# First expert layer as three float32r products with its weights loaded and split per tile, three query buffers, and written-out expert loops

## The chip, the cores and the metric

The kernel runs on one core of a Trainium2 chip. Its engines are TensorE (PE in the profile, with PEld for its weight loads), VectorE (DVE), ScalarE (ACT), GpSimd (POOL) and SyncE (SP), each with an instruction queue of its own that runs in order, and they meet at semaphores. The metric is the device time of one execution in microseconds, the median of three runs. All times below are microseconds (us) unless another unit stands with them.

## What is computed

One transformer layer on x of 4096 rows by 256, with an attention and a mixture of eight experts, of which each row takes two:

```
h = layernorm(x) * (1 + ca) + sa
x = x + ga * attention(h)              # 16 heads of 16; key <= query + 128
h = layernorm(x) * (1 + cb) + sb
scores = h @ gate_w + gate_b           # 8 experts, the top 2 of each row
hid = relu(einsum('td,edf->etf', h, W1) + b1[:, None, :])   # 256 -> 1024
y = einsum('etf,efd->etd', hid, W2) + b2[:, None, :]        # 1024 -> 256
x = x + gb * einsum('te,etd->td', combine, y)
```

All inputs are float32. W1 and W2 hold eight experts of 1 MB each.

## The kernel before

The program runs five stages one after the other: attention_inputs with the projections (to about 130 us), score_shifts and row_maxima (to 193), attention (to 1284), route (to 1460) and experts (to 2046), and then a copy of the sums to the output.

**attention** goes over 32 tiles of 512 queries: four groups of four heads (g), eight tiles each, r counting both. SP loads a tile's queries (load_stack into q_rows, two halves by turns, L983 to L985), then waits on q_in until they have landed (L986), and at tile 3 of a group loads the keys of the next group (L987 to L990). Before the load of tile r it waits for `turned` of tile r-2 (L983). TensorE makes scores of keys and queries (L1009), later the products of probabilities and values (L1026), and, one tile behind, four transposes of the finished output (L1038), which raise `turned`. ScalarE takes the exponentials (L1107), GpSimd cuts the edge of the mask (L1092), VectorE copies and divides.

**route** goes over eight chunks of 512 rows: normalise, score, choose two experts, count each row's place in its expert's queue, and scatter the normalised rows (rt_xs, L1473) to a queue in DRAM, eight scatters a chunk. SP's load() brings the chunk's attention output and x, stores sums, and loads a share of W1, one expert of 1 MB a chunk (L1279), which stays in SBUF for all eight experts; load_w2 brings W2. GpSimd adds the bias to x (L1343).

**experts** goes over 71 tiles of 128 queue rows, each of one expert. What each engine does for a tile t:

- SP: loads the tile of rows (value load L1715, DMA L1716), once the tile two before has been transposed and its meta columns have been read. The last three experts of W2 are loaded at the start of the stage (L1721).
- TensorE: first_layer(t) in fp32, two halves of 512 columns by two halves of the inner 256 (L1760; each fp32 product stands as two instructions, so eight rows); turn_rows(t+1), two transposes (L1750); second_layer(t-1), eight products (L1779); turn_hidden(t), eight transposes (L1771).
- VectorE: copies half of the hidden layer (L1853), modulates the transposed rows into xT (modulate, L1829), reads the meta columns of the row tile (read_meta, L1838 to L1845: the row's share and where its answer goes, four steps on one column), and makes the answer (L1858 to L1871: denominator, reciprocal, output plus bias b2, times share and gate).
- ScalarE: one exponential (L1808), the other half of the hidden layer (L1811), eight relu (L1814).
- GpSimd: scatter-adds the answer to the sums in DRAM (L1739). A scatter waits for the one before to have landed.

The loops over tiles are hardware loops (over_queue, with Fori, two tiles a pass). The order on each engine is the order of the code.

Of the kernel before, what the change touches and what calls it, by code (L numbers as in the profile page):

```python
# [857 lines left out]
def attention(nc, dram, keep):  # L858

    with ExitStack() as ctx:  # L860
# [21 lines left out]
        q_rows = sb("at_q_rows", [STACK, 2 * GH * C], BF16)  # L882
# [11 lines left out]
        q_in = sem("at_q_in")  # L894
# [77 lines left out]
        def _(sp):  # L972
# [5 lines left out]
            for r in range(TILE_COUNT):  # L978
                g, tile = r // NC, r % NC
                half = r % 2  # L980

                if r >= 2:
                    sp.wait_ge(turned, r - 1)  # L983
                load_stack(sp, q_rows[:, half * GH * C:(half + 1) * GH * C].rearrange("r (h s) -> r h s", h=GH),
                           dram["q_parts"], Q_TERM, slice(g * GH, (g + 1) * GH), slice(tile * C, (tile + 1) * C), q_in)  # L985
# [5 lines left out]
            sp.wait_ge(k_in, G * K_IN)  # L991

        @block.tensor
        def _(pe):
            def scores(g, tile, n, c):
# [3 lines left out]
                k_at, q_at = (g % 2) * GH * S, ((g * NC + tile) % 2) * GH * C  # L999
# [63 lines left out]
            for c, (g, tile, n) in enumerate(order):  # L1063
                if n == 0:
                    if tile == 0:
                        pe.wait_ge(k_in, (g + 1) * K_IN)
                    pe.wait_ge(q_in, (g * NC + tile + 1) * Q_IN)
# [63 lines left out]
def route(nc, dram, keep):  # L1131
# [6 lines left out]
    with ExitStack() as ctx:  # L1138
# [117 lines left out]
        W1_SHARE = E // NC  # L1256
# [5 lines left out]
        def _(sp):  # L1262
# [5 lines left out]
            def load(c, u, it):  # L1268
# [378 lines left out]
def experts(nc, dram, keep):  # L1647


    with ExitStack() as ctx:  # L1650
# [6 lines left out]
        def sem(name):  # L1657
            return ctx.enter_context(nc.semaphore(name))

        ident, mod_cols, w1, w2, b1, b2, owner = (  # L1660
            keep[n] for n in ("ident", "mod_cols", "w1", "w2", "b1", "b2", "owner"))
# [10 lines left out]
        xT = sb("ex_xT", [P, KD, P], F32)  # L1672
        h = sb("ex_h", [P, FF * P], F32)
# [9 lines left out]
        w2_in = sem("ex_w2_in")  # L1683
        x_turned = sem("ex_x_turned")
# [15 lines left out]
        def over_queue(eng, body, done=0):  # L1700

            with eng.Fori(done, (TILES - 1) // 2) as it:
                for u in range(2):
                    body(it * 2 + (u + 1), (u + 1) % 2, it)

        @block.sync
        def _(sp):
            sp.sem_inc(x_turned, 2)

            def load(tile, u):  # L1710

                sp.wait_ge(x_turned, tile + 1)
                if not isinstance(tile, int) or tile >= 2:
# [8 lines left out]
            load(2, 0)  # L1722
            over_queue(sp, lambda tile, u, it: load(tile, u), done=1)
            load(TILES, TILES % 2)
            sp.wait_ge(x_in[TILES % 2], 16 * ((TILES + 1) // 2))
# [7 lines left out]
        def _(pool):  # L1733
            for tile in range(TILES):
                pool.wait_ge(y_ready, tile + 3)
# [9 lines left out]
        def _(pe):  # L1745
# [7 lines left out]
            def first_layer(tile):  # L1753
                e = pe.value_load(owner[0:1, bass.ds(tile, 1)], min_val=0, max_val=E - 1)
                pe.wait_ge(xT_ready, tile + 2)
                for i in range(HALVES):

                    pe.wait_ge(h_copied[i], tile + 1)
                    for k in range(KD):
                        ins = nc.tensor.matmul(ps_h[i][:], xT[:, k, :],  # L1760
                                               w1[:, bass.ds(e, 1), k, i * C:(i + 1) * C].rearrange(
                                                   "p a f -> p (a f)"), start=k == 0, stop=k == KD - 1)
                    ins.then_inc(hidden[i], 1)
                return e
# [196 lines left out]
```

## Time and profile before

| | |
|---|---|
| median of three runs | 2066.1 us (2063.37 to 2066.82) |
| the profiled execution | 2067.55 us |
| its span, first to last instruction | 2065.8 us |
| TensorE busy | 1828.7 us (89% of the span) |
| ScalarE busy | 1337.1 us (65%) |
| VectorE busy | 466.4 us (23%) |
| GpSimd busy | 290.1 us (14%) |
| exponentials of attention, L1107 | 1023.4 us busy, 756 of them |
| second layer, L1779 | 258.7 us busy, 1136 rows |

Busy shares are means over five stages that differ, so the profile is read stage by stage: the busy times of a stretch tell which engine never stops there, the timeline of one tile tells how long each step takes and what released it, and the chain of waits tells what stood on the path that ended last. In a timeline row the columns are start, duration, engine, line, operation, output and inputs, shape and count; the bracket gives the engine's idle time ahead of the row and what ended it. A granted clock (PEclk) of 1.00 is TensorE's full speed.

### The profile page before, as it was taken

Reading aid. Unit: us, or ns where it says so; the run is one execution under the profiler, and the core shown is the slowest. Engines: PE = TensorE matmul, PEld = TensorE weight load, DVE = VectorE, ACT = ScalarE, POOL = GpSimd, SP = SyncE. Lnnn points to the kernel's source line nnn. Section 1 sums busy time; section 2 is a strip of 40 time slices with the busy share of each in tenths; the row PEclk is TensorE's granted clock in tenths of the full one; section 3 lists DMA queues with packets and bytes.
Section 4 is the critical chain, followed back from the end, with each engine's and each line's share of the span. In section 5 each row is a group of like instructions: output and inputs, shape, how many; then the busy total and the mean of one; then the engine's idle time right before and its main releaser. Section 6 shows DMA issues by size and latency. Waiting matters only on the chain. (4 is left out here: it accounts for less than half of the span.)

```text
span 2065.8 us, 47120 instructions
## 1 busy us (share of the span) xinstructions
PE 1828.7 (89%) x18425; PEld 949.3 (46%) x18426; DVE 466.4 (23%) x1368; ACT 1337.1 (65%) x1649; POOL 290.1 (14%) x333
## 2 busy tenths in 40 slices
PE   4944999999999999999999998664599999999995
PEld 3832333333333333333333332554376767666673
DVE  4954000000000000000000000445133333333331
ACT  3723999998899989999899998222233333333331
POOL 1000101001000010000111000356112121212111
PEclk8975999999999999999999999765799999999998
DMA  4464400003100003000000000962412122122223
GB/s 138 155 158 101 88 10 10 10 10 66 40 10 10 10 17 81 18 9 10 15 20 18 10 2 10 347 247 83 122 31 34 33 33 33 33 33 33 33 33 97
DMA packets 84274, 116.10 MB, mean 56 GB/s; under 512 B 9484, under 2 KB 76108, under 8 KB 83532
## 3 DMA queue, kind: packets, MB, share of 16 engines
q1 hardware_dynamic: 67064, 90.97, 15.5%
q0 software_dynamic: 13296, 17.80, 5.0%
q10 hardware_dynamic: 3760, 5.03, 0.9%
q8 instruction: 126, 2.06, 0.4%
q14 instruction: 28, 0.23, 0.0%
HBM read 73.03 MB, written 40.74 MB: 55 GB/s over the span
## 5 line engine op out<-in xcount | busy, mean ns | idle before, releaser
L1107 ACT ACTIVATE at_probs<-at_scores 128x1536 f32<-128x1536 f32 (+2 forms) x756 | 1023.4, 1436 | 62.7 <-PE at_scores L1009 57.4
L1009 PE MATMUL at_scores<-at_q_rows,kept_k_rows 99*32 99x512 bf16 (+3 forms) x9920 | 621.1, 363 | 38.3 <-ACT at_probs L1107 16.9
L1026 PE MATMUL at_out<-at_probs,kept_v 128*17 128x512 f32 (+3 forms) x4832 | 587.9, 565 | 5.0 <-DVE at_out_T L1120 4.9
L1009 PEld LDWEIGHTS at_scores<-at_q_rows,kept_k_rows 99*32 99x32 bf16 x9920 | 239.6, 97 | 564.3 <-ACT at_probs L1107 342.3
L1814 ACT ACTIVATE ex_hT<-ex_ps_hT,kept_b 128x128 f32<-128x128 f32 x568 | 154.2, 383 | 376.0 <-PE ex_ps_hT L1771 376.0
L1779 PE MATMUL ex_ps_y<-kept_w,ex_hT 128*128 x1136 | 258.7, 381 | 2.4 <-ACT ex_hT L1814 2.4
L1760 PE MATMUL ex_ps_h<-kept_w,ex_xT 128*128 x568 | 259.9, 601 | 0.9 <-DVE ex_xT L1829 0.9
L1120 DVE COPY at_out_T<-at_out 128x512 f32<-128x512 f32 x32 | 22.1, 692 | 972.1 <-PE at_out L1026 972.1
L1092 POOL TENSOR_SCALAR_AFFINE_SELECT at_probs<-at_probs 128x512 f32<-128x512 f32 (+2 forms) x156 | 83.0, 541 | 1014.7 <-ACT at_probs L1107 1013.3
L1779 PEld LDWEIGHTS ex_ps_y<-kept_w,ex_hT 128*128 128x128 f32 x1136 | 211.7, 191 | 28.6 <-issue 2.7
L1026 PEld LDWEIGHTS at_out<-at_probs,kept_v 128*17 128x17 f32 x4832 | 127.9, 98 | 130.3 <-DVE at_out_T L1120 19.9
L1739 POOL DMA_INDIRECT sums<-ex_y,ex_answer_to x71 | 110.7, 1560 | 486.9 <-DVE ex_y L1871 486.9
L1760 PEld LDWEIGHTS ex_ps_h<-kept_w,ex_xT 128*128 128x128 f32 x568 | 104.2, 194 | 105.8 <-issue 105.8
L1853 DVE COPY ex_h<-ex_ps_h 128x512 f32<-128x512 f32 x71 | 49.2, 692 | 229.5 <-PE ex_ps_h L1760 229.5
L1771 PE MATMUL ex_ps_hT<-kept_ident,ex_h 128*128 128x128 f32 x568 | 74.5, 275 | 0.0
L1353 POOL DMA_INDIRECT queue<-rt_xs,rt_row_int x64 | 65.6, 1026 | 56.5 <-DVE rt_row_int L1585 39.5
L1771 PEld LDWEIGHTS ex_ps_hT<-kept_ident,ex_h 128*128 128x128 f32 x568 | 67.3, 142 | 7.0
L1829 DVE TENSOR_SCALAR ex_xT<-ex_ps_x,kept_mod_cols 128x128 f32<-128x128 f32 x144 | 51.9, 403 | 21.3 <-PE ex_ps_x L1750 21.3
L1392 PE MATMUL rt_ps_o<-rt_wo,rt_aT 128*128 128x256 f32 x128 | 45.5, 533 | 9.1 <-ACT rt_aT L1463 9.1
L1750 PE MATMUL ex_ps_x<-kept_ident,ex_x_tile 128*128 128x128 f32 x144 | 28.1, 277 | 28.5 <-DMA ex_x_tile<-queue 24.7
L1750 PEld LDWEIGHTS ex_ps_x<-kept_ident,ex_x_tile 128*128 128x128 f32 x144 | 20.5, 144 | 66.2 <-issue 61.6
L1811 ACT COPY ex_h<-ex_ps_h 128x512 f32<-128x512 f32 x71 | 45.0, 634 | 4.2 <-PE ex_ps_h L1760 4.2
(220 smaller groups left out, 963.0 us busy)
## 6 DMA issues: line engine op xcount, KB each, us to landing
kept_w<-in_W SPq DMA_DIRECT2D x16, 1024.0 KB, 11.3
ex_x_tile<-queue SPq DMA_DIRECT2D x72, 129.5 KB, 2.1
k_parts<-kparts SPq DMA_DIRECT2D x8, 768.0 KB, 3.7
q_parts<-qparts SPq DMA_DIRECT2D x8, 768.0 KB, 3.7
at_q_rows<-q_parts SPq DMA_DIRECT2D x32, 192.0 KB
kept_k_rows<-k_parts SPq DMA_DIRECT2D x4, 1120.0 KB
x_rows<-in_x SPq DMA_DIRECT2D x4, 1024.0 KB, 13.9
kept_k_rows<-k_parts SPq DMA_DIRECT2D x8, 512.0 KB
```

Of the source, the lines that this page charges most:

```text
L1009: ins = nc.tensor.matmul(ps_s[b:b + CT, c % 2, at:at + part], k_rows[:, k + b:k + b + CT], q_rows[:, q:q + part], start=True, stop=True)
L1026: ins = nc.tensor.matmul(ps_o[h * CT:h * CT + HD + 1, first:C], v[:, kb, g * GH + h, :], probs[:, slot, column:column + width], start=i == ...
L1092: nc.gpsimd.affine_select(out=part, in_=part, compare_op=ALU.is_ge, fill=0.0, base=0, pattern=pattern, channel_multiplier=-1).then_inc(mas ...
L1107: nc.scalar.activation(probs[:, c % RING, 0:width], ps_s[:, c % 2, 0:width], ACT.Exp).then_inc(exped, 1)
L1353: pool.indirect_dma_start(dram["queue"], bass.IndirectOffsetOnAxis(ap=row_int[:, u, j, i:i + 1], axis=0), xs[:, u, j, :], None).then_inc(s ...
L1739: pool.indirect_dma_start(dram["sums"], bass.IndirectOffsetOnAxis(ap=answer_to[:, tile:tile + 1], axis=0), y[:, tile % 2, :], None, comput ...
L1760: ins = nc.tensor.matmul(ps_h[i][:], xT[:, k, :], w1[:, bass.ds(e, 1), k, i * C:(i + 1) * C].rearrange("p a f -> p (a f)"), start=k == 0, ...
L1771: ins = nc.tensor.transpose(ps_hT[:, f, :], h[:, f * P:(f + 1) * P], ident[:])
L1779: ins = nc.tensor.matmul(ps_y[u][:, 0:D], hT[:, f, :], w2[:, bass.ds(e, 1), f, :].rearrange("p a d -> p (a d)"), start=f == 0, stop=f == F ...
L1814: nc.scalar.activation(hT[:, f, :], ps_hT[:, f, :], ACT.Relu, bias=b1[:, bass.ds(e * FF + f, 1)]).then_inc(rectified, 1)
L1829: ins = nc.vector.tensor_scalar(xT[:, k, :], ps_x[:, k * P:(k + 1) * P], mod_cols[:, 6 + k:7 + k], mod_cols[:, 4 + k:5 + k], ALU.mult, ALU ...
L1853: nc.vector.tensor_copy(h[:, C:2 * C], ps_h[1][:]).then_inc(h_copied[1], 1)
```

## The change

Three things are changed.

1. attention has three query buffers with a semaphore each. SP waits, from the fourth tile on, for the scores of the tile that last read the buffer (`scored`), in place of the transposes, and no longer waits after each load that it has landed. The load of the next group's keys, which stands behind the load of tile 3 on SP, is no longer behind that wait either.
2. route no longer loads W1, and W1 has no room of its own for all experts.
3. experts loads the W1 of a tile's expert anew for each tile, into two buffers, and splits it on chip: ScalarE rounds it to float32r (w1_high), VectorE and GpSimd subtract that from the full weights, half each (w1_low). The rows are split the same way on VectorE (xT_high, xT_low); modulate moves to ScalarE. The first layer is then, for each half of the columns, high by high, high by low and low by high, twelve float32r products of 512 columns in place of four fp32 ones. The loops over tiles are written out.

The core of the diff:

```diff
-                if r >= 2:
-                    sp.wait_ge(turned, r - 1)
...
-                sp.wait_ge(q_in, (r + 1) * Q_IN)
+                u = r % Q_BUFFERS
+                if r >= Q_BUFFERS:
+                    done = r - Q_BUFFERS + 1
+                    sp.wait_ge(scored, chunk_base(done // NC, done % NC))
...
                 if tile == 3 and g + 1 < G:
 
                     sp.wait_ge(k_in, (g + 1) * K_IN)
                     load_keys(g + 1)
...
-                share = bass.ds(c * W1_SHARE, W1_SHARE)
-                sp.dma_start(keep["w1"][:, share].rearrange("p e k f -> p (e k) f"),
-                             dram["W1"][share].rearrange("e (k p) f -> p (e k) f", p=P)
-                             ).then_inc(keep["weights_in"], 16)
...
+            def load_w1(tile, u):
+                if tile >= 2:
+                    for k in range(KD):
+                        sp.wait_ge(w1_rest[k], tile - 1)
+                e = sp.value_load(owner[0:1, bass.ds(tile, 1)], min_val=0, max_val=E - 1)
+                sp.dma_start(w1[:, u], dram["W1"][bass.ds(e, 1)].rearrange("e (k p) f -> p (e k) f", p=P)
+                             ).then_inc(w1_in[u], 16)
+
+            load_w1(0, 0)
             load(0, 0)
             load(1, 1)
+            load_w1(1, 1)
             for e in range(E - 3, E):
...
+            for tile in range(2, TILES):
+                load(tile, tile % 2)
+                load_w1(tile, tile % 2)
...
+            def rest(tile):
+                pool.wait_ge(w1_rounded, tile + 1)
+                if tile >= 2:
+                    pool.wait_ge(hidden[HALVES - 1], tile - 1)
+                nc.gpsimd.tensor_tensor(w1_low[:, tile % 2, 1], w1[:, tile % 2, 1], w1_high[:, tile % 2, 1],
+                                        ALU.subtract).then_inc(w1_rest[1], 1)
+            rest(0)
+            rest(1)
             for tile in range(TILES):
+                if tile + 2 < TILES:
+                    rest(tile + 2)
                 pool.wait_ge(y_ready, tile + 3)
...
+                    for n, (x_part, w) in enumerate(((xT_high, w1_high), (xT_high, w1_low), (xT_low, w1_high))):
+                        for k in range(KD):
+                            ins = nc.tensor.matmul(ps_h[i][:], x_part[:, k, :], w[:, u, k, cols],
+                                                   start=n == 0 and k == 0, stop=n == 2 and k == KD - 1)
...
+            def round_w1(tile):
+                act.wait_ge(w1_in[u], (tile // 2 + 1) * 16)
+                if tile >= 2:
+                    act.wait_ge(hidden[HALVES - 1], tile - 1)
+                    for k in range(KD):
+                        act.wait_ge(w1_rest[k], tile - 1)
+                nc.scalar.copy(w1_high[:, u], w1[:, u]).then_inc(w1_rounded, 1)
...
                 nc.scalar.copy(h[:, 0:C], ps_h[0][:]).then_inc(h_copied[0], 1)
+                if tile + 1 < TILES:
+                    modulate(tile + 1)
+                if tile + 2 < TILES:
+                    round_w1(tile + 2)
                 act.wait_ge(h_turned, tile + 1)
...
+            def split_x(tile):
+                dve.wait_ge(xT_full, tile + 1)
+                if tile >= 1:
+                    dve.wait_ge(hidden[HALVES - 1], tile)
+                nc.vector.tensor_copy(xT_high[:], xT[:]).then_inc(xT_rounded, 1)
+                dve.wait_ge(xT_rounded, tile + 1)
+                nc.vector.tensor_tensor(xT_low[:], xT[:], xT_high[:], ALU.subtract).then_inc(xT_ready, 1)
...
                 copy_hidden(tile)
-                modulate(tile + 1)
-                if not isinstance(tile, int) or tile + 1 < TILES:
+                if tile + 1 < TILES:
+                    split_x(tile + 1)
                     read_meta(tile + 1, 1 - u)
+                if tile + 2 < TILES:
+                    rest(tile + 2)
                 answer(tile - 1, 1 - u)
```

The first rest(tile) above is GpSimd's, round_w1 is ScalarE's, split_x VectorE's. VectorE has a rest(tile) like GpSimd's, on the first half of the inner 256 and with w1_rest[0].

SP's queue in the expert loop, one tile, before (the value load and the DMA of the rows, then the loop's branch):

```order
L1715 TENSOR_LOAD kept_row_of_tile [waits ex_meta_read,ex_x_turned]
L1715 ISA x2
L1716 ISA
L1716 DMA ex_x_tile<-queue 128x259
L1702 UNCONDITIONAL_BRANCH
```

and after, the same tile (ex_w is the buffer of W1, kept_owner the expert of each tile):

```order
L1718 TENSOR_LOAD kept_row_of_tile [waits ex_meta_read,ex_x_turned]
L1718 ISA x2
L1719 ISA
L1719 DMA ex_x_tile<-queue 128x259
L1726 TENSOR_LOAD kept_owner [waits ex_w1_rest_1,ex_w1_rest_0]
L1726 ISA x2
L1727 ISA
L1727 DMA ex_w<-in_W 128x2x1024
```

Behind each load of rows now stands a load of weights with two waits of its own, and each load of weights stands behind the load of rows of the same tile.

VectorE's queue in the expert loop, one step, before (copy of the hidden half, modulate, the meta columns, then the answer):

```order
L1853 COPY ex_h<-ex_ps_h 128x512 [waits ex_hidden_1]
L1829 TENSOR_SCALAR ex_xT<-ex_ps_x,kept_mod_cols 128x128 [waits ex_x_turned]
L1829 TENSOR_SCALAR ex_xT<-ex_ps_x,kept_mod_cols 128x128
L1838 TENSOR_SCALAR ex_sign<-ex_x_tile,kept_owner_of 128x1
L1840 TENSOR_SCALAR ex_padding<-ex_x_tile,kept_spill 128x1
L1843 SCALAR_TENSOR_TENSOR ex_lead<-ex_sign,ex_x_tile 128x1 [waits ex_meta_step]
L1845 SCALAR_TENSOR_TENSOR ex_answer_to<-ex_padding,ex_x_tile 128x1
L1858 TENSOR_LOAD kept_owner [waits ex_meta_read]
L1858 ISA x2
L1861 TENSOR_SCALAR ex_den<-ex_grown 128x1 [waits ex_grown_ready]
```

and after:

```order
L1912 COPY ex_h<-ex_ps_h 128x512 [waits ex_hidden_1]
L1881 CAST ex_xT_high<-ex_xT 128x256 [waits ex_hidden_1,ex_xT_full]
L1883 TENSOR_TENSOR ex_xT_low<-ex_xT,ex_xT_high 128x256 [waits ex_xT_rounded]
L1897 TENSOR_SCALAR ex_sign<-ex_x_tile,kept_owner_of 128x1
L1899 TENSOR_SCALAR ex_padding<-ex_x_tile,kept_spill 128x1
L1902 SCALAR_TENSOR_TENSOR ex_lead<-ex_sign,ex_x_tile 128x1 [waits ex_meta_step]
L1904 SCALAR_TENSOR_TENSOR ex_answer_to<-ex_padding,ex_x_tile 128x1
L1889 TENSOR_TENSOR ex_w_low<-ex_w,ex_w_high 128x1024 [waits ex_hidden_1,ex_w1_rounded,ex_meta_read]
L1917 TENSOR_LOAD kept_owner
L1917 ISA x2
L1920 TENSOR_SCALAR ex_den<-ex_grown 128x1 [waits ex_grown_ready]
```

The two steps of modulate have left this queue, the split of the rows stands in their place, and the subtraction of the weights stands between the meta columns and the answer.

## Rows read from the trace of the kernel before

**Rows 1.** expert loop busy: us, PE, PEld, DVE, ACT, POOL, PEclk, DMA, GB/s

```profile
1482.00:2044.00 562.00, 559.55 (x2383) 391.25 (x2382) 213.88 (x768) 191.11 (x698) 109.19 (x70) 1.00 0.20 32
```

**Rows 2.** timeline, one tile's TensorE work in the expert loop

```profile
1688.86 0.38 PE L1750 MATMUL ex_ps_x<-kept_ident,ex_x_tile 128*128 128x128 f32 x2
...
1693.41 3.60 PE L1760 MATMUL ex_ps_h<-kept_w,ex_xT 128*128 x8
...
1696.85 0.38 PE L1750 MATMUL ex_ps_x<-kept_ident,ex_x_tile 128*128 128x128 f32 x2
```

**Rows 3.** timeline, TensorE's float32r products in the prologue

```profile
76.16 0.71 PE L345 MATMUL ps_q<-hT_high,wq_high 128*128 128x512 f32 x2
...
79.00 3.62 PE L356 MATMUL ps_v<-wv,hT 128*128 128x256 f32 x16
```

**Rows 4.** groups by line: busy and mean ns, idle time before

```profile
L576 ACT ACTIVATE sh_square_k<-sh_high_k 128x2048 bf16<-128x2048 bf16 x4 | 7.6, 1910 | 34.0 <-DMA sh_high_k<-k_parts 34.0
...
L443 DVE TENSOR_TENSOR hT_low<-hT,hT_high 128x1024 fp32r<-128x1024 f32 x8 | 9.8, 1219 | 7.2 <-ACT hT L280 7.2
```

**Rows 5.** timeline of the route stage, GpSimd and VectorE

```profile
1372.31 2.35 POOL L1343 TENSOR_TENSOR rt_x_now<-rt_x_now,rt_bo_gated 128x1024 f32<-128x1024 f32 x1
...
1372.50 0.19 DVE L1575 TENSOR_TENSOR rt_rank<-rt_ps_r,rt_queue_end 128x32 f32<-128x32 f32 x1 [2.01 <-PE rt_ps_r L1422]
...
1372.80 1.91 DVE L1581 TENSOR_TENSOR rt_equal<-rt_rank,kept_w 128x32 f32<-128x32 f32 x1
```

**Rows 6.** chain of waits, SP at the start of the experts

```profile
1459.28 0.27 SPq L1715
...
1460.01 0.37 SPq L1716
```

**Rows 7.** timeline, VectorE's and GpSimd's steps of a tile

```profile
1690.76 0.16 DVE L1843 SCALAR_TENSOR_TENSOR ex_lead<-ex_sign,ex_x_tile 128x1 f32 x1
...
1691.94 0.15 DVE L1861 TENSOR_SCALAR ex_den<-ex_grown 128x1 f32 x1 [0.91 <-DVE ex_answer_to L1845]
...
1692.95 0.42 DVE L1868 TENSOR_TENSOR ex_y<-ex_ps_y,kept_b 128x256 f32<-128x256 f32 x1 [0.66 <-PE ex_ps_y L1779]
...
1693.41 0.48 DVE L1871 SCALAR_TENSOR_TENSOR ex_y<-ex_y,ex_share,kept_gates 128x256 f32<-128x256 f32 x1
...
1694.17 1.57 POOL L1739 DMA_INDIRECT sums<-ex_y,ex_answer_to  x1 [6.42 <-DVE ex_y L1871]
```

**Rows 8.** page, DMA issues: count, KB each, median us to landing

```profile
ex_x_tile<-queue SPq DMA_DIRECT2D x72, 129.5 KB, 2.1
...
k_parts<-kparts SPq DMA_DIRECT2D x8, 768.0 KB, 3.7
...
sums<-ex_y,ex_answer_to POOLq DMA_INDIRECT x71, 3.8
```

**Rows 9.** one line's landings, L1721 (three loads of W2)

```profile
DMA to landing us min/median/max: 6.6/9.1/11.3
```

**Rows 10.** timeline of attention: first tile of groups 0, 1 and 3

```profile
207.09 7.00 ACT L1107 ACTIVATE at_probs<-at_scores 128x1536 f32<-128x1536 f32 x5 [1.00 <-PE at_scores L1009]
...
474.74 2.75 PE L1009 MATMUL at_scores<-at_q_rows,kept_k_rows 99*32 99x384 bf16 x56 [3.88 <-DMA at_q_rows<-q_parts]
...
476.27 2.79 ACT L1107 ACTIVATE at_probs<-at_scores 128x1536 f32<-128x1536 f32 x2 [5.70 <-PE at_scores L1009]
...
1023.81 2.80 ACT L1107 ACTIVATE at_probs<-at_scores 128x1536 f32<-128x1536 f32 x2 [4.96 <-PE at_scores L1009]
```

**Rows 11.** timeline of attention, behind a load of keys

```profile
521.27 1.04 PE L1009 MATMUL at_scores<-at_q_rows,kept_k_rows 99*32 99x512 bf16 x7 [2.93 <-issue]
```

**Rows 12.** busy times of the route stage, columns as in group 1

```profile
1284.00:1460.00 176.00, 94.74 (x497) 79.47 (x497) 78.56 (x303) 39.88 (x67) 87.02 (x83) 0.64 0.60 213
```

**Rows 13.** waits: us in total, times, longest

```profile
ACT rt_xs L1473 <- DMA queue<-rt_xs,rt_row_int: 41.5, 6, 10.5
```

**Rows 14.** chain of waits, last load of W2

```profile
1462.65 11.35 DMA kept_w<-in_W
```

More of the change, by code:

```diff
@@ L893, in attention @@
         k_in = keep["k_in"]
-        q_in = sem("at_q_in")
+        q_in = [sem(f"at_q_in_{u}") for u in range(Q_BUFFERS)]
         ready = sem("at_ready")
@@ L991, in _ @@
             sp.wait_ge(k_in, G * K_IN)
+            for u in range(Q_BUFFERS):
+                sp.wait_ge(q_in[u], Q_IN * len(range(u, TILE_COUNT, Q_BUFFERS)))
         @block.tensor
@@ L1683, in experts @@
         w2_in = sem("ex_w2_in")
+        w1_in = [sem(f"ex_w1_in_{u}") for u in range(2)]
+        w1_rounded = sem("ex_w1_rounded")
+        w1_rest = [sem(f"ex_w1_rest_{k}") for k in range(KD)]
+        xT_full = sem("ex_xT_full")
+        xT_rounded = sem("ex_xT_rounded")
         x_turned = sem("ex_x_turned")
@@ L1698, in experts @@
         block = ctx.enter_context(nc.Block())
[L1700 to L1704, printed above, removed]
         @block.sync
@@ L1791, in tile_steps @@
             def tile_steps(tile, u, it):
-                first_layer(tile)
-                turn_rows(tile + 1, 1 - u, it + 2)
+                first_layer(tile, u)
+                if tile + 1 < TILES:
+                    turn_rows(tile + 1, 1 - u, it + 2)
                 second_layer(tile - 1, 1 - u)
                 turn_hidden(tile)
-            over_queue(pe, tile_steps)
+            for tile in range(1, TILES):
+                tile_steps(tile, tile % 2, (tile - 1) // 2)
             second_layer(TILES - 1, (TILES - 1) % 2)
@@ L1815, in tile_steps @@
                                          bias=b1[:, bass.ds(e * FF + f, 1)]).then_inc(rectified, 1)
-            tile_steps(0)
-            over_queue(act, lambda tile, u, it: tile_steps(tile))
+            round_w1(0)
+            modulate(0)
+            round_w1(1)
+            for tile in range(TILES):
+                tile_steps(tile)
         @block.vector
@@ L1824, in _, with rest @@
             dve.sem_inc(y_ready, 2)
-            def modulate(tile):
-                dve.wait_ge(x_turned, tile + 3)
-                for k in range(KD):
-                    ins = nc.vector.tensor_scalar(xT[:, k, :], ps_x[:, k * P:(k + 1) * P], mod_cols[:, 6 + k:7 + k],
-                                                  mod_cols[:, 4 + k:5 + k], ALU.mult, ALU.add)
-                ins.then_inc(xT_ready, 1)
+            def split_x(tile):
[5 more added lines that the diff above has]
+                nc.vector.tensor_tensor(xT_low[:], xT[:], xT_high[:], ALU.subtract).then_inc(xT_ready, 1)
+            def rest(tile):
+                dve.wait_ge(w1_rounded, tile + 1)
+                if tile >= 2:
+                    dve.wait_ge(hidden[HALVES - 1], tile - 1)
+                nc.vector.tensor_tensor(w1_low[:, tile % 2, 0], w1[:, tile % 2, 0], w1_high[:, tile % 2, 0],
+                                        ALU.subtract).then_inc(w1_rest[0], 1)
             META = 3
@@ L1864, in answer @@
                 dve.wait_ge(out_done, tile + 1)
-                if not isinstance(tile, int) or tile >= 2:
+                if tile >= 2:
                     dve.wait_ge(y_added, tile * 16 - 16)
```

73 lines of the change are left out of this document (39 added, 34 removed).

## Prediction

> **What bounds the kernel now.** I read the stages first, then in the expert stage the engine that is never idle, then the gaps of the attention stage. In the expert loop TensorE is busy 559.55 of 562 us at a granted clock of 1.00, while VectorE, ScalarE and GpSimd are busy 214, 191 and 109 us [rows 1]. A tile takes 7.99 us (1688.86 to 1696.85), of which the first layer's eight fp32 passes take 3.44 (1693.41 to 1696.85) [rows 2]. So whatever shortens TensorE's row pays in full, until another chain of work takes longer than TensorE's row. The attention stage is bound by ScalarE's exponentials, which stop for 5 to 6 us at three places [rows 10].
>
> **First layer on TensorE.** Removed: 3.44 us a tile. Added: 12 float32r products on 512 columns. The prologue has the same form: 12 of them run from 76.16 to 79.00 [rows 3], 2.84 us. I take that; with 3.44 as the end at which nothing is gained, and no reason for less than 2.84. TensorE's own period becomes 7.99 - 3.44 + 2.84 = 7.39 us. The written-out loops issue the same TensorE work in the same order.
>
> **The new chain for weights.** W1 now comes once per tile, and a buffer is free for tile t+4 only when both subtractions for tile t+2 are done. GpSimd's subtraction stands ahead of a scatter and behind the last scatter on its queue, VectorE's ahead of the answer that the scatter needs. That closes a loop which returns after two tiles:
> scatter(t-1), GpSimd subtract(t+2), SP's load of x and of W1 for t+4, ScalarE's rounding(t+4), VectorE subtract(t+4), answer(t+1), scatter(t+1). Its links:
> - GpSimd subtracts 128x1024 in fp32: 2.35, as the same shape takes in the route stage [rows 5].
> - Before SP comes to W1 it must issue the x tile (the queue is in order), and that waits for read_meta, VectorE's [128x1] steps with two operands in SBUF. In the route stage a VectorE operation with two SBUF operands that began 0.49 after GpSimd's subtract took 1.91 and ended at 1374.71, 0.05 after GpSimd's end at 1374.66; its neighbour of the same 128x32 shape with one operand in PSUM took 0.19 [rows 5]. I take it that read_meta is held the same way: it ends 0.15 after the subtraction, one step of 0.16 without it [rows 7].
> - SP: 0.73 from the end of its wait to the issue of x, and 0.37 for the issue itself [rows 6]: 1.10; then 0.73 again up to the issue of W1.
> - Landing of 1 MB. No row shows this load. 129.5 KB take 2.1 and 768 KB take 3.7 [rows 8], which is 2.5 ns per KB and gives 4.4 for 1024 KB alone, the lower end. The upper end is 6.6, the first of three 1 MB loads of W2 in one burst [rows 9]. The loop's present traffic keeps the DMA engines 0.20 busy [rows 1], 1.6 us of a tile's 8; if half of it falls into the load, 0.8 more: 5.1 is my estimate, nearer to the lower end since no second large load is in flight with it.
> - ScalarE rounds 128x2048: 1.9, taken from a bf16 row of that shape; VectorE subtracts 128x1024: 1.22 [rows 4].
> - The answer: 0.35 for the denominator and its reciprocal, 0.94 for the two steps on y (1692.95 to 1693.89); 0.28 to the scatter's start and 1.57 for it [rows 7].
> - Six handovers between engines at 0.05, as at the held step's end [rows 5]: 0.3.
> Sum: 2.35 + 0.15 + 1.10 + 0.73 + 5.1 + 1.9 + 1.22 + 1.29 + 1.85 + 0.3 = 15.99 us for two tiles, **8.0 a tile**, against 7.99 now. The register load ahead of the answer shows 0.91 of idle time today [rows 7]; I cost it at nothing because the 1.22 of the subtraction ahead of it on VectorE covers it. Without that cover the loop is 16.9, 8.45 a tile, +31 us.
> So the 0.60 us that TensorE saves per tile I expect to be idle time on TensorE, and the loop to run at the pace of the weights. 68 tiles x 0.01 = +1 us.
>
> What else is moved in this stage: modulate goes to ScalarE (two 128x128 steps, about 0.7 in place of VectorE's), and the rounding stands on ScalarE's queue ahead of the eight relu of the same tile. If W1(t+2) is late, the relu wait behind it, and second_layer(t) behind them. ScalarE then has 191 / 70.3 = 2.7 us a tile of today [rows 1] plus 1.9 plus 0.7, 5.3 of 8; VectorE 3.0 of today, less 0.7, plus two steps of 0.48 or less for split_x (the 128x256 form of [rows 7]) and 1.22, and what it is held, under 7. Neither is the bound. The scatter itself waits for the rows of the scatter before, which land 3.8 after their issue [rows 8], well inside a period.
>
> "SBUF — State Buffer", section "Who interferes with whom", in the Trainium skill speaks against this change: a VectorE instruction with two SBUF inputs and a GpSimd instruction that reads SBUF exclude each other for the whole of an instruction, and the one that issued first keeps the port. The trace agrees for 128x32 (1.91 in place of 0.19), and no run here shows it for a 128x1 step. By that rule the loop is 8.0 a tile; were the small steps exempt, it would be the 7.39 of the first rival.
>
> **Attention.** SP loads the queries of a group's first tile only after the transposes of two tiles before, and at three boundaries TensorE waits for that DMA (3.88 at 474.74) and ScalarE behind it 5.70 to 4.96 [rows 10]. With a third buffer, released when the scores have read it, those loads are there a tile ahead. What is left is the gap of the same place in group 0, where they were in time: 1.00 [rows 10]. The three gaps are 16.3 together (5.70, one of about 5.6, 4.96): 16.3 - 3.0 = **-13**. Ends: -18 if the refill after each gap shrinks as well, -8 if the keys of the next group, now issued some two tiles earlier, cost more than today. A stall of 2.93 on "issue" stands behind such a key load [rows 11], and it can come at another place.
>
> **Route.** Eight loads of 1 MB go. The stage moves 213 GB/s x 176 us = 37 MB [rows 12], so they are 0.21 of it. ScalarE waits 41.5 us there for scattered rows [rows 13]; 0.21 of that is 9, the gain if the wait is all bandwidth, and 0 is the other end. I take -4.
>
> **Start of the experts.** Today 3 MB of W2 land 11.35 after the last issue [rows 14], and the second tile waits for them. Landings of 6.6 and 11.3 for the first and third [rows 9] with issues 0.6 apart are 2.9 us a MB. Two loads of W1 now stand ahead on SP: 5.8, less what runs before W2 would be wanted. I take +5 (3 to 6).
>
> **Sum.** The profiled run took 2067.55 (span 2065.8), 1.45 above the median of 2066.1; I add the differences to the median. 2066.1 - 13 - 4 + 5 + 1 = **2055**. Its own range is set by the landing: 4.4 gives 7.65 a tile and 2055 - 24; 6.1 gives 8.5 and 2055 + 34. So 2031 to 2089.
>
> **Rivals.**
> - The small steps of read_meta aren't held. Then x is issued under GpSimd's subtraction, 0.15 and 1.10 leave the loop, which falls to 14.74, 7.37 a tile, and TensorE's 7.39 binds again: 68 x 0.60 = 41 less than today in the loop, 2066.1 - 12 - 41 = **2013**. For it: they read one column, and no row shows such a step held. Against it: the held row is only 32 wide, and its length did not depend on its own work. A landing near 4 would lead here too.
> - The load is slower than I think, and the kernel gets slower. Place: the landing of W1 beside x, scatter-add and rows of the other buffer. At 6.6 [rows 9] the loop is 17.49, 8.74 a tile, 68 x 0.75 = +51: 2066.1 - 12 + 51 = **2105**. It decides from 8.17 a tile on, a landing of 5.4, where the loop has eaten the 12 us of the other stages. For it: 5.4 is only 0.3 above my estimate, and every new wait (the register load, a scatter that is held by a VectorE step) adds to the same chain. Against it: 768 KB in 3.7 on this chip.
> - The change doesn't do what it says. The three gaps of attention stay, as TensorE waits for keys rather than queries, or the written-out loops wait for instructions behind the weight loads as at [rows 11]; the loop as forecast: about **2068**.
> A lower clock is no rival of its own: the route stage has TensorE busy 95 of 176 us at a granted 0.64 [rows 12], but in the forecast TensorE stays busy over nine tenths of the loop.
>
> **How the numbers follow.** Forecast 0.50, small steps free 0.23, slow landing 0.22, no effect 0.05. The range takes in the first rival and the forecast's upper end, and leaves out most of the slow case: **2008 to 2092**. 0.2% is 4.1 us, about what a measurement of this kernel can tell from no change. The forecast's range lies below 2062 for two thirds (0.32), within 4 us for 0.06, and above 2070 for 0.12. With the rivals: faster 0.32 + 0.23 + 0.02 = 0.57, the same 0.06 + 0.03 = 0.09 and slower 0.12 + 0.22 = 0.34.
>
> **What would show it.** In the profile after: 12 float32r products in about 2.84 a tile; between them and the transposes an idle time on TensorE of about 0.6, released by the subtractions; read_meta's two-operand steps at 1 us or more in place of 0.16, ending with GpSimd's subtract; W1's median landing, which decides alone between 2013, 2055 and 2105; attention's gaps of 5 to 6 at about 1. The forecast is wrong if TensorE isn't idle in the loop (the chain is shorter), if TensorE waits for anything but weights, or if the scatter, not the subtraction, is held.

## The result, and the profile after

The changed kernel takes 2087.97 us (median; 2087.74 to 2091.47) against 2065.83 for the one before: 1.0111 times as long, with a 95% interval of 1.0097 to 1.0125. It is 22 us slower; 2055 was predicted. The time lies inside the stated range, near its upper end, but on the other side of no change. The profiled execution took 2091.47 with a span of 2089.8, 24.0 more than the span before.

By stages, read from the first and last rows of each in the two traces, the 24.0 come about like this: the exponentials of attention last 1074.3 in place of 1080.6 (-6.3); from their last one to the first transposes of the experts 185.2 in place of 183.1 (+2.1); from there to the first second layer 23.3 in place of 19.2 (+4.1); from the first second layer to the last 587.3 in place of 562.8 (**+24.5**); what lies ahead and behind adds +0.4 and -0.8. So the loss is made in the expert loop: 70 tiles in 587.3 are 8.39 a tile, where the kernel before has 562.8 / 70 = 8.04 with the loop's ends and 7.99 inside.

The busy times of the same stretch as [rows 1], with the same columns:

```profile
1482.00:2044.00 562.00, 518.21 (x2559) 426.82 (x2559) 489.87 (x806) 354.65 (x873) 263.04 (x134) 1.00 0.52 157
```

TensorE is no longer unbroken: 44 us of idle time. The granted clock stays at 1.00, so none of it is a lower clock. VectorE's busy time has more than doubled, to 490. The groups by line tell what it was busy with (columns: busy us, mean ns | idle time before and what ended it):

```profile
L1881 DVE CAST ex_xT_high<-ex_xT 128x256 fp32r<-128x256 f32 x71 | 233.6, 3290 | 45.2 <-ACT ex_xT L1845 45.1
...
L1751 POOL TENSOR_TENSOR ex_w_low<-ex_w,ex_w_high 128x1024 fp32r<-128x1024 f32 x71 | 206.7, 2911 | 29.6 <-ACT ex_w_high L1839 29.6
...
L1787 PE MATMUL ex_ps_h<-ex_w_high,ex_xT_high 128*128 128x512 f32 x284 | 97.5, 425 | 45.2 <-DVE ex_xT_low L1883 38.4 <-DVE ex_w_low L1889 5.1 <-issue 1.8
```

A cast of 128x256 elements takes 3.29 us, longer than GpSimd's subtraction of four times as many. TensorE's idle time stands ahead of the first product of a tile and is ended by xT_low, the subtraction of the rows right behind that cast, in 66 cases with 38.4 us together; the 5.1 us that end with the weights are a single wait, at the first tile. By the list of waits (us in total, times, longest):

```profile
PE ex_ps_h L1787 <- DVE ex_xT_low L1883: 38.4, 66, 0.8
```

One round of the loop in the timeline:

```profile
1703.67 0.37 SPq L1727 DMA_DIRECT2D ex_w<-in_W  x1
...
1704.77 1.57 POOL L1763 DMA_INDIRECT sums<-ex_y,ex_answer_to  x1 [4.20 <-DVE ex_y L1930]
1705.42 3.49 DVE L1881 CAST ex_xT_high<-ex_xT 128x256 fp32r<-128x256 f32 x1 [0.32 <-ACT ex_xT L1845]
1705.80 2.94 POOL L1751 TENSOR_TENSOR ex_w_low<-ex_w,ex_w_high 128x1024 fp32r<-128x1024 f32 x1
...
1708.62 1.90 ACT L1839 CAST ex_w_high<-ex_w 128x2048 fp32r<-128x2048 f32 x1 [3.24 <-DMA ex_w<-in_W]
1708.94 0.43 DVE L1883 TENSOR_TENSOR ex_xT_low<-ex_xT,ex_xT_high 128x256 fp32r<-128x256 f32 x1
...
1709.42 0.73 PE L1787 MATMUL ex_ps_h<-ex_w_high,ex_xT_high 128*128 128x512 f32 x2 [0.55 <-DVE ex_xT_low L1883]
...
1709.72 0.15 DVE L1904 SCALAR_TENSOR_TENSOR ex_answer_to<-ex_padding,ex_x_tile 128x1 uint32<-128x1 f32 x1
...
1710.62 1.23 DVE L1889 TENSOR_TENSOR ex_w_low<-ex_w,ex_w_high 128x1024 fp32r<-128x1024 f32 x1 [0.74 <-DVE ex_answer_to L1904]
...
1711.83 0.67 SPq L1727 DMA_DIRECT2D ex_w<-in_W  x1
...
1712.59 0.48 DVE L1930 SCALAR_TENSOR_TENSOR ex_y<-ex_y,ex_share,kept_gates 128x256 f32<-128x256 f32 x1
...
1713.35 1.57 POOL L1763 DMA_INDIRECT sums<-ex_y,ex_answer_to  x1 [4.61 <-DVE ex_y L1930]
1713.90 3.57 DVE L1881 CAST ex_xT_high<-ex_xT 128x256 fp32r<-128x256 f32 x1 [0.23 <-ACT ex_xT L1845]
1714.38 2.93 POOL L1751 TENSOR_TENSOR ex_w_low<-ex_w,ex_w_high 128x1024 fp32r<-128x1024 f32 x1
```

The cast of 1705.42 begins while the scatter is still running and ends at 1708.91, 0.17 behind GpSimd's end at 1708.74; the next begins at 1713.90 and ends at 1717.47, 0.16 behind 1717.31. Both casts begin ahead of GpSimd's subtraction by the records (0.38 and 0.48) and are held all the same. Whatever stands behind the cast on VectorE's queue, xT_low, read_meta, the weights' subtraction and the answer, waits as well.

The same rows walk the loop of two tiles that the prediction set up, from one load of W1 to the next but one. The chain of waits has the loads (start, us, what):

```profile
1703.67 4.93 DMA ex_w<-in_W
...
1708.62 1.26 ACT ex_w_high L1839
...
1709.95 0.27 SPq L1718
...
1711.83 5.19 DMA ex_w<-in_W
...
1720.42 4.79 DMA ex_w<-in_W
```

Between them the profile infers a shorter way, from the rounding to SP's load of rows (L1718) after 1.26 of its 1.90 us. SP has no wait for the rounding there: its queue waits for read_meta and the transposes, and the point where the profile leaves the rounding, 1709.88, is where read_meta ends in the timeline (1709.72 + 0.15). So the walk goes by the queues and their waits. From 1703.67 to 1720.42 it is 16.75: landing 4.93, rounding 1.90 with 0.12 of handovers, VectorE's subtraction 1.23, the answer to 1713.07 1.22, to the scatter 0.28, the scatter to GpSimd's next subtraction 1.03, that one 2.93, from its end at 1717.31 to the end of read_meta at 1718.44 1.13, and from there to the next issue of W1 1.98. 16.75 / 2 = 8.38 a tile, which is the loop. In the rounds from 1500 on, single distances between loads of W1 lie anywhere from 7.83 to 9.04, while two successive ones add up to 16.75 at the median, as a loop of two tiles would have it.

The landing that decided between the cases is as forecast, 4.9 at the median (page, DMA issues), against 5.1:

```profile
ex_w<-in_W SPq DMA_DIRECT2D x71, 1024.0 KB, 4.9
```

In attention the first tile of group 1, as in [rows 10], and two new gaps:

```profile
477.85 7.00 ACT L1112 ACTIVATE at_probs<-at_scores 128x1536 f32<-128x1536 f32 x5 [0.99 <-PE at_scores L1013]
...
226.69 0.58 PE L1013 MATMUL at_scores<-at_q_rows,kept_k_rows 99*32 99x256 bf16 x5 [4.76 <-issue]
...
227.31 1.45 ACT L1112 ACTIVATE at_probs<-at_scores 128x1536 f32<-128x1536 f32 x1 [5.06 <-PE at_scores L1013]
...
766.36 1.45 ACT L1112 ACTIVATE at_probs<-at_scores 128x1536 f32<-128x1536 f32 x1 [4.58 <-PE at_scores L1013]
```

The wait for queries has gone from 5.70 to 0.99, as predicted. But behind each load of keys, 14 to 15 us after its issue (208.30, 477.49 and 747.00), TensorE stops on "issue", time in which it waits for nothing that the profile shows: 4.76, 2.62 and 4.52 us. Before there were two such stops over 1 us, the 2.93 of [rows 11] and one of 1.98. The gaps over 1 us on ScalarE at these three places are 19.6 us together; before, they were 7.9 at two places.

### The profile page after: what moved, and what is told of

The parts are those of the page before. It is cut to its first block and busy times, and to the rows that moved or that the text cites. A ratio compares the mean times of both kernels' runs of the same rounds, so it can differ in the third digit from the quotient of the medians.

```text
span 2089.8 us, 46765 instructions
## 1 busy us (share of the span) xinstructions
PE 1806.9 (86%) x18707; PEld 1006.0 (48%) x18707; DVE 766.3 (37%) x1436; ACT 1517.2 (73%) x1861; POOL 461.3 (22%) x404
## 3 DMA queue, kind: packets, MB, share of 16 engines
q1 hardware_dynamic: 84056, 156.91, 24.5%
## 5 line engine op out<-in xcount | busy, mean ns | idle before, releaser
L1112 ACT ACTIVATE at_probs<-at_scores 128x1536 f32<-128x1536 f32 (+2 forms) x756 | 1022.6, 1436 | 57.5 <-PE at_scores L1013 52.1
L1839 ACT CAST ex_w_high<-ex_w 128x2048 fp32r<-128x2048 f32 x71 | 135.1, 1903 | 241.1 <-DMA ex_w<-in_W 241.1
L1881 DVE CAST ex_xT_high<-ex_xT 128x256 fp32r<-128x256 f32 x71 | 233.6, 3290 | 45.2 <-ACT ex_xT L1845 45.1
L1751 POOL TENSOR_TENSOR ex_w_low<-ex_w,ex_w_high 128x1024 fp32r<-128x1024 f32 x71 | 206.7, 2911 | 29.6 <-ACT ex_w_high L1839 29.6
L1787 PE MATMUL ex_ps_h<-ex_w_high,ex_xT_high 128*128 128x512 f32 x284 | 97.5, 425 | 45.2 <-DVE ex_xT_low L1883 38.4
L1889 DVE TENSOR_TENSOR ex_w_low<-ex_w,ex_w_high 128x1024 fp32r<-128x1024 f32 x71 | 87.0, 1225 | 39.8 <-DVE ex_answer_to L1904 30.4
L1787 PE MATMUL ex_ps_h<-ex_w_low,ex_xT_high 128*128 128x512 f32 x284 | 89.6, 397 | 0.0
L1787 PE MATMUL ex_ps_h<-ex_w_high,ex_xT_low 128*128 128x512 f32 x284 | 89.2, 396 | 0.0
L1787 PEld LDWEIGHTS ex_ps_h<-ex_w_high,ex_xT_high 128*128 128x128 f32 x284 | 48.8, 191 | 67.8 <-DVE ex_xT_low L1883 54.1
```

The lines of the kernel that those rows point to most:

```text
L1112: nc.scalar.activation(probs[:, c % RING, 0:width], ps_s[:, c % 2, 0:width], ACT.Exp).then_inc(exped, 1)
L1751: nc.gpsimd.tensor_tensor(w1_low[:, tile % 2, 1], w1[:, tile % 2, 1], w1_high[:, tile % 2, 1], ALU.subtract).then_inc(w1_rest[1], 1)
L1787: ins = nc.tensor.matmul(ps_h[i][:], x_part[:, k, :], w[:, u, k, cols], start=n == 0 and k == 0, stop=n == 2 and k == KD - 1)
L1839: nc.scalar.copy(w1_high[:, u], w1[:, u]).then_inc(w1_rounded, 1)
L1881: nc.vector.tensor_copy(xT_high[:], xT[:]).then_inc(xT_rounded, 1)
L1889: nc.vector.tensor_tensor(w1_low[:, tile % 2, 0], w1[:, tile % 2, 0], w1_high[:, tile % 2, 0], ALU.subtract).then_inc(w1_rest[0], 1)
```

## Experiments

Theory A: GpSimd's subtraction holds VectorE, in the order on the two queues, and this makes the loop. Rivals: the steps of one column aren't held (then the reordering frees the loop); the load of 1 MB a tile is the bound by itself; a shorter loop of one tile exists beside the one predicted. The attention's part is tested apart.

**e1_meta_first**: read_meta ahead of split_x. The added wait is for the transposes, which split_x used to cover.

```diff
+                dve.wait_ge(x_turned, tile + 3)
                 step.inc(nc.vector.tensor_scalar(sign[:]
...
+                    read_meta(tile + 1, 1 - u)
                     split_x(tile + 1)
-                    read_meta(tile + 1, 1 - u)
```

> The changed kernel with one swap on VectorE: read_meta(t+1) stands ahead of split_x(t+1) in place of behind it. Theory A (only split_x's cast is held by GpSimd's subtraction, the steps on one column are not): in the trace of the changed kernel read_meta ends 1.13 us after GpSimd's subtraction and SP's load of x follows it; both leave the loop, 16.75 - 1.13 - 1.10 = 14.5 us for two tiles, under TensorE's 7.39 a tile, so about 7.45 a tile in place of 8.37 and about 2025 us. Rival B (the two-operand steps of read_meta are held as well, as the prediction had it): they end with GpSimd's subtraction wherever they stand ahead of the cast, the loop keeps at least 15.7 for two tiles: 7.9 to 8.4 a tile, 2055 to 2088 us. Rival C (the weights' load is the bound by itself): no change, 2088.

2052.11 us, 0.9929 of before (0.9910 to 0.9948), a loop of 553.7 / 70 = 7.91 a tile. This is rival B by its 7.9 to 8.4 a tile; the time lies 3 us under its 2055 to 2088. The groups by line, and one round:

```profile
L1903 DVE SCALAR_TENSOR_TENSOR ex_lead<-ex_sign,ex_x_tile 128x1 f32<-128x1 f32 x71 | 197.1, 2776 | 2.4
...
L1881 DVE CAST ex_xT_high<-ex_xT 128x256 fp32r<-128x256 f32 x71 | 22.4, 315 | 25.7 <-ACT ex_xT L1845 23.3
```

```profile
1702.41 3.38 DVE L1903 SCALAR_TENSOR_TENSOR ex_lead<-ex_sign,ex_x_tile 128x1 f32<-128x1 f32 x1
1702.84 2.92 POOL L1751 TENSOR_TENSOR ex_w_low<-ex_w,ex_w_high 128x1024 fp32r<-128x1024 f32 x1
...
1705.71 0.15 DVE L1905 SCALAR_TENSOR_TENSOR ex_answer_to<-ex_padding,ex_x_tile 128x1 uint32<-128x1 f32 x1
```

The hold has moved from the cast, now 0.32 us, to the first step with two SBUF operands, of one column: 2.78 in place of 0.16 [rows 7]. So the prediction's reading was right that such small steps are held, and its first rival, 2013, falls. The one-operand steps ahead of it, sign and padding, keep their 0.20. The steps that lead to the next load of W1 now end at 1705.86, 0.10 behind GpSimd's subtraction, in place of 1.13: 1.03 less in every loop of two tiles, 35 us over 34 of them, and the loop is 33.6 us shorter than in the changed kernel. That it stops at 7.91, and not at TensorE's 7.39, this run doesn't explain.

**e5_w1_small**: from the third tile on the load is cut to 64 of the 1024 columns, 64 KB; the rest of the weights stays that of the first two tiles.

```diff
-                sp.dma_start(w1[:, u], dram["W1"][bass.ds(e, 1)].rearrange("e (k p) f -> p (e k) f", p=P)
+                cols = slice(0, FF * P if tile < 2 else 64)
+                sp.dma_start(w1[:, u, :, cols],
+                             dram["W1"][bass.ds(e, 1), :, cols].rearrange("e (k p) f -> p (e k) f", p=P)
                              ).then_inc(w1_in[u], 16)
```

> The changed kernel with the load of W1 cut from the third tile on to 64 of its 1024 columns (64 KB in place of 1 MB); rounding, subtractions and products work on what lies in the buffer, so the rest of the weights is that of the first two tiles. Theory A (one loop of two tiles through landing, rounding, subtraction, answer, scatter and GpSimd's subtraction): the landing falls from 4.9 us to about 2.1, the loop from 16.75 to 13.9 us, below TensorE's 7.39 a tile: 7.4 to 7.5 and about 2025 us. Rival G (a loop of one tile without the landing: GpSimd's subtraction holds VectorE's cast, behind it x_low, the meta columns, VectorE's subtraction, the answer, the scatter, and GpSimd's next subtraction; from the trace of the changed kernel 8.57 us with 0.74 us of waiting for the rounding in it): 7.8 to 7.9 a tile, about 2055 us. Rival C (the traffic of 1 MB a tile slows everything else): under 2025.

2050.0 us, 0.9909 of before (0.9889 to 0.9930), 7.86 a tile: rival G, and not theory A's 7.4. The landing, and one round from issue to issue of W1:

```profile
ex_w<-in_W SPq DMA_DIRECT2D x69, 64.0 KB, 1.9
```

```profile
1701.81 0.37 SPq L1728 DMA_DIRECT2D ex_w<-in_W  x1
...
1703.50 3.23 DVE L1883 CAST ex_xT_high<-ex_xT 128x256 fp32r<-128x256 f32 x1 [0.37 <-ACT ex_xT L1847]
1703.64 2.94 POOL L1753 TENSOR_TENSOR ex_w_low<-ex_w,ex_w_high 128x1024 fp32r<-128x1024 f32 x1
...
1707.74 1.23 DVE L1891 TENSOR_TENSOR ex_w_low<-ex_w,ex_w_high 128x1024 fp32r<-128x1024 f32 x1
...
1709.68 0.37 SPq L1728 DMA_DIRECT2D ex_w<-in_W  x1
...
1710.47 1.56 POOL L1765 DMA_INDIRECT sums<-ex_y,ex_answer_to  x1 [3.90 <-PE ex_ps_h L1789]
...
1711.51 2.91 POOL L1753 TENSOR_TENSOR ex_w_low<-ex_w,ex_w_high 128x1024 fp32r<-128x1024 f32 x1
```

With the load 3 us shorter the loop is still 7.87 (1701.81 to 1709.68), and it closes over one tile, without the weights: GpSimd's subtraction 2.94 holds the cast; behind it xT_low and read_meta 1.16; VectorE's subtraction 1.23; the answer 1.22; 0.28 to the scatter; 1.04 of it; and GpSimd's next subtraction. 2.94 + 1.16 + 1.23 + 1.22 + 0.28 + 1.04 = 7.87. The profile's own chain takes another way round in the same time, from the held cast by xT_low, TensorE's first layer, the transposes and modulate back to the cast. It counts the hold as the cast's own time, and the cast would end with GpSimd's subtraction also if it began a little earlier, so I take the walk above; no run separates the two. Both are longer than TensorE's row of 7.39, so no landing however short would have brought the first rival's pace. In the changed kernel the two loops stand close together, 7.87 and 16.75 / 2 = 8.38, and the longer one is seen.

**e2_all_dve**: both halves of the subtraction on VectorE.

```diff
-                if tile + 2 < TILES:
-                    rest(tile + 2)
                 pool.wait_ge(y_ready, tile + 3)
...
-                nc.vector.tensor_tensor(w1_low[:, tile % 2, 0], w1[:, tile % 2, 0], w1_high[:, tile % 2, 0],
-                                        ALU.subtract).then_inc(w1_rest[0], 1)
+                for k in range(KD):
+                    nc.vector.tensor_tensor(w1_low[:, tile % 2, k], w1[:, tile % 2, k], w1_high[:, tile % 2, k],
+                                            ALU.subtract).then_inc(w1_rest[k], 1)
```

> The changed kernel with GpSimd's half of the subtraction given to VectorE, so that GpSimd only scatters. Theory A (GpSimd's subtraction behind the scatter, and VectorE held by it, make the loop): the cast falls from 3.3 us to under 1, VectorE has some 6.2 us of work a tile, TensorE's 7.39 binds: about 7.45 a tile and 2025 us. Rival C (the 1 MB load a tile and its landing of 4.9 us are the bound): the landing stays, and so does the period, 8.3 a tile and 2085 us.

2017.84 us, 0.9766 of before (0.9750 to 0.9783), somewhat better than theory A's 2025; rival C falls, since the same 1 MB a tile is still loaded, with the same landing of 4.9. VectorE was given work, and its busy time fell: the cast's row and the loop's busy times, columns as in [rows 4] and [rows 1]:

```profile
L1870 DVE CAST ex_xT_high<-ex_xT 128x256 fp32r<-128x256 f32 x71 | 25.9, 364 | 31.2 <-ACT ex_xT L1834 30.5
```

```profile
1482.00:1980.00 498.00, 498.00 (x2590) 428.86 (x2589) 360.90 (x885) 369.86 (x889) 107.60 (x69) 1.00 0.63 178
```

TensorE is busy for all of 498 us; 515.9 / 70 is 7.37 a tile, the 7.39 that the prediction worked out for TensorE alone.

**e3_pool_early**: GpSimd subtracts one tile earlier in its queue.

```diff
+            rest(2)
             for tile in range(TILES):
-                if tile + 2 < TILES:
-                    rest(tile + 2)
+                if tile + 3 < TILES:
+                    rest(tile + 3)
```

> The changed kernel with GpSimd's subtraction one place earlier in its queue: rest(t+3) ahead of scatter(t), so that it can follow the rounding at once, in place of waiting for the answer and the scatter ahead of it. Theory A: the scatter and the answer leave the loop of the weights; VectorE's and GpSimd's subtractions exclude each other (1.2 + 2.4 to 2.9 behind the rounding), two tiles of the loop take about 4.95 + 1.9 + 4.0 + 2.0 = 12.9, TensorE binds with 7.4 to 7.7 a tile: 2022 to 2043 us. Rival D (what matters is that VectorE is held at all, wherever the subtraction stands): the answer is held in place of the cast, 8.2 to 8.6 a tile, 2077 to 2104 us.

The four runs lie between 2048.68 and 2100.25, one at the lower end and three at the upper, so there is no verdict. The three lie in rival D's range, the fourth in neither. In the profiled one, of the upper three, VectorE's subtraction takes 2.89 at the mean where it took 1.23, and xT_low 0.97: the hold has only moved to other steps, though not to the answer that rival D named. In the same trace the loads of W1 are 7.7 apart at the mean from 1500 to 1685 and 8.9 after that, by turns long and short (11.64, 4.26, 15.00, 4.91): the program falls from one phase into another. Why is open.

**e7_attention_only**, **e4_keys_spread** and **e8_attention_keys**: attention apart. e7 is the kernel before with the change of attention alone. In e4 (on the changed kernel) and e8 (on e7) the keys are loaded one head at a time:

```diff
-                if tile == 3 and g + 1 < G:
-
-                    sp.wait_ge(k_in, (g + 1) * K_IN)
-                    load_keys(g + 1)
+                if 3 <= tile < 3 + GH and g + 1 < G:
+                    sp.wait_ge(k_in, (1 + g * GH + tile - 3) * K_IN)
+                    load_keys(g + 1, tile - 3)
```

> The kernel before with only the change of attention (three query buffers, the wait on the scores). By the traces attention ended 5.9 us earlier in the changed kernel (the three waits for queries gone, -13 to -16, the stalls behind the keys grown by 8 to 10): 2060 us. If the prediction's -13 was right and the rest was lost elsewhere: 2053.

2057.33 us, 0.9942 (0.9924 to 0.9960), 12 less than the 2069.32 of the runs of before beside it. The expected 2060 and 2053 were meant against 2066, so they stand for 6 and 13 less, and it is the second that is met. Its stalls behind the keys were smaller than in the changed kernel's trace, gaps over 1 us of 13.5 in place of 19.6, with the same code of attention: their size differs from run to run. Six traces have this code (the changed kernel, e1, e2, e3, e5, e7); their exponentials last 6.3 to 12.5 less than the 1080.6 of before, 10.5 in e7, and the changed kernel's own trace has the least.

> The changed kernel with the keys of the next group loaded one head at a time, behind the query loads of tiles 3, 4, 5 and 6, in place of all four heads behind that of tile 3. Theory E (the stalls of 4.76, 2.62 and 4.52 us on issue in attention are TensorE waiting for instructions that come behind the 3 MB of keys): they go, ScalarE's gaps over 1 us fall from 19.6 us in three places to under 4, and the kernel takes about 2088 - 15 = 2073 us. Rival F (the stalls come from where the instruction stream stands, not from the load): they stay, 2088 us.

2075.14 us, 1.0038 (1.0024 to 1.0052) where the changed kernel has 1.0111: 0.73%, 15 us, as theory E had it. In its trace attention is 21 us shorter than in the changed kernel's, and the expert loop, with the same code, 8 longer (595.5), so the total alone would not tell. ScalarE's wait for scores, by the list of waits (us in total, times, longest):

```profile
ACT at_probs L1111 <- PE at_scores L1012: 31.4, 62, 4.2
```

It was 57.4 before and 52.1 after the change. No gap over 1 us is left but the first tile's, so rival F falls. The DMA queues, read by windows of 1 us, show more. A queue for instructions, q8, otherwise moves a packet of some 16 KB every 4 to 11 us. In the changed kernel's trace none moves from 206 to 223, from 478 to 492 and from 747 to 762, behind each load of keys, and each stop of TensorE begins within 2 us of the packet that ends the pause (at 221.9, 492.8 and 761.2). In e4 no pause there is longer than 10. This fits theory E, without proving it: the trace doesn't say whose instructions q8 brings, and the kernel before has pauses of 15 to 18 behind its three loads of keys with a stop behind two of them.

> The kernel before with the change of attention and the keys loaded one head at a time. The stalls behind the keys are gone (19.6 us of gaps over 1 us in the changed kernel, 7.9 in the kernel before): 6 us less by the query buffers and 13 to 15 less by the keys, 2046 us.

2041.53 us, 0.9873 (0.9855 to 0.9891), 28 less than before where 20 was expected. Attention now lasts 1053.3 against 1080.6.

**e9_written_out**: the expert loops of the kernel before written out.

```diff
-            with eng.Fori(done, (TILES - 1) // 2) as it:
+            for it in range(done, (TILES - 1) // 2):
```

> The kernel before with nothing changed but its expert loops written out. TensorE's row is unbroken in both (559.55 of 562 us busy before), so the prediction's price of nothing holds: within 4 us of before. If the written-out code stalls on its instructions as attention does behind the keys: some us more.

2067.64 us, 0.9999 (0.9984 to 1.0014): nothing, as priced.

**e6_best** and **e10_w2_late**: both findings together, then TensorE's wait for W2 put later.

> The changed kernel with both findings: both halves of the subtraction on VectorE, and the keys of the next group loaded one head at a time. If the two are independent, 2018 (subtraction on VectorE) less the 13 to 15 us that the keys gave: about 2004 us, a ratio of 0.970 to before. If the loop falls out of TensorE's pace again with another phase: 2012 or more.

1999.12 us, 0.9667 of before (0.9650 to 0.9685); the two add up, and a little more (0.970 expected).

```diff
             first_layer(0, 0)
-            pe.wait_ge(w2_in, 16 * 3)
             turn_rows(1, 1, 1)
...
+                if tile == 1:
+                    pe.wait_ge(w2_in, 16 * 3)
                 second_layer(tile - 1, 1 - u)
```

> The kernel with the whole subtraction on VectorE and the keys one head at a time, in which TensorE waits for the last three experts of W2 only ahead of the first second layer, no longer ahead of the second tile's transposes. In the trace of that kernel it waits 1.2 us there, and the second tile's first layer stands behind it; the gain is 1 to 4 us: 1995 to 1998 us. If the weights of the second tile are later still, nothing: 1999.

1997.61 us, 0.9655 (0.9635 to 0.9675). Its interval overlaps that of e6, so the last step isn't told from nothing. Either of the two beats both kernels, by 3.3 to 3.5% (before) and 4.4 to 4.5% (changed).

## Why the prediction was wrong

**The direction** came out wrong by one step: "it ends 0.15 after the subtraction, one step of 0.16 without it". The mechanism was named and is shown (e1, e2): GpSimd's subtraction holds VectorE. But the prediction let the hold begin at read_meta. It begins two steps earlier, at the cast, which it costed at "0.48 or less" in VectorE's total without asking where a hold of it would fall in the loop. Behind the held cast xT_low and all of read_meta still have to run, and the term of 0.15 measured 1.13. The walk measures 16.75 where the sum had 15.99, 0.76 more: this term alone is +0.98, and the rest cancel to -0.2. Times 68 / 2 tiles, 0.76 is 26 us on top of the +1 that was forecast; the loop came out at +24.5. The experiment for this term is e1: there the steps end 0.10 behind the subtraction, close to the forecast's 0.15, and the loop takes 7.91 a tile where 8.0 was forecast. That e1's total, 2052, lies near 2055 is in part luck, since the other stages came out otherwise than forecast.

A sign that the prediction itself named came up: "if TensorE waits for anything but weights". TensorE waited for the split rows (38.4 us). Its other sign, read_meta's two-operand steps at 1 us or more, stayed out in the changed kernel (0.16 and 0.15), since the cast ahead of them had taken the hold; e1 brought it out.

In the Trainium skill, the same section of "SBUF — State Buffer" ("Who interferes with whom") that the prediction weighed says that copies and casts, too, may run in a mode that takes the shared port, under conditions that it refers to another page for. The trace agrees: 3.29 us for the cast under GpSimd's subtraction, 0.36 without it (e2). By that sentence the hold could have begun at the cast, and the loop come out near the 16.75 seen. The prediction also took from there that the one that issued first keeps the port. By the recorded starts the casts shown began first and were the ones held; since GpSimd's recorded spans overlap, the true order is not certain.

**The loop of one tile** was not seen at all. The prediction asked which way the weights go round and stopped there. VectorE's and GpSimd's queues close a shorter loop without the weights, 7.87, which e5 laid bare. So the first rival (TensorE's pace of 7.39 after all) and the second (decided by the landing alone) were both set up on the wrong lever: "W1's median landing, which decides alone between 2013, 2055 and 2105" is false, since the landing came out at 4.9 and the loop at 8.39.

**Terms that held.** TensorE's float32r row: 7.37 a tile in e2, against 7.39. Landing 4.9 against 5.1. GpSimd's subtraction reads 2.92 in place of 2.35, but it overlaps the scatter ahead of it by some half a microsecond in the records; the two together are 1.03 + 2.93 = 3.96 against 1.57 + 2.35 = 3.92. The steps of one column are held (e1). The register load ahead of the answer is hidden: 0.15 of the denominator starts with the end of VectorE's subtraction. Written-out loops cost nothing (e9).

**Attention**: the three waits went, as costed, but the 13 turned into 6.3 in this trace and into 12 in e7; over six traces it is 6.3 to 12.5, from below the stated -8 up to nearly the -13. The end at which "the keys of the next group, now issued some two tiles earlier, cost more than today" is what happened: the stalls on issue grew with the earlier load. That the load in one piece makes them is shown by e4 and e8; why they grew, and why they differ from run to run, isn't.

**Route and start**: -4 became +2.1, +5 became +4.1 in this trace. ScalarE's wait for scattered rows was 41.5 before [rows 13] and 33.9 after, but the stage did not become shorter; across the runs of both kinds it lasted 183 to 187. So W1's share of the traffic wasn't what set its length.

## What to carry to other kernels

When work is split between VectorE and GpSimd, ask of each VectorE step that will meet the GpSimd one, casts included, whether it can be held, and charge all that stands behind it on the queue: handing GpSimd half of a subtraction cost more than the whole of it on VectorE (8.39 a tile against 7.37). Look for every loop that a new wait closes, also the short ones within two queues, before costing the longest. And a large load that nothing waits for can still stop an engine, here together with a pause on an instruction queue; the same bytes in four parts did not.

## What the runs showed of the hardware that was not expected

A VectorE cast of 128x256 from float32 to float32r, one operand in SBUF, took 0.31 to 0.36 us at the mean where it was not held (e1 to e3) and 3.2 to 3.6 in the rounds shown beside GpSimd's 128x1024 subtraction, of which it outlasted the end by 0.15 to 0.17, though by the records it began 0.1 to 0.5 ahead of it. A step of one column with two operands in SBUF took 2.78 at the mean in place of 0.16 (e1). Loads of keys of 3 MB were followed, 14 to 15 us after their issue, by stops of TensorE of 2.6 to 4.8 us that the profile puts down to issue, beside pauses of 14 to 17 us on an instruction queue, and by no stop over 1 us when they came in four parts.
